# Sparse cross attention, 64 batches: one more pipeline stage, with a new order of work on all engines

## The reference, cut to what matters

```python
q = split_heads(x @ w_q);  k, v = split_heads(text @ w_k), split_heads(text @ w_v)
out_text = softmax(q k^T / 4) v
out_ip   = softmax(q k_ip^T / 4 + mask_ip) v_ip      # mask_ip: a box per query, 8 columns
out = (merge(out_text) + merge(out_ip)) @ w_out + b_out + x
```

## Time and profile before

| | us |
|---|---|
| median of 3 runs | 1598.76 (1596.06 to 1602.39) |
| profiled execution | 1604.02 |
| its span, first to last instruction | 1602.1 |
| PE busy | 1385.2 (86%) |
| PE weight loads busy | 1266.7 (79%) |
| DVE busy | 1173.1 (73%) |
| ACT busy | 848.4 (53%) |
| POOL busy | 806.3 (50%) |
| mean granted TensorE clock | 0.959 |

### The profile page before, as it was taken

The page is one execution under the profiler, slowest core; times in us unless marked ns, Lnnn a source line. Parts: engine busy times, 40 slices in busy tenths (PEclk is TensorE's granted clock), DMA queues, the critical chain, the costliest instruction groups (busy, mean ns, idle before and its releaser), DMA issues.

```text
span 1602.1 us, 48578 instructions
## 1 busy us (share of the span) xinstructions
PE 1385.2 (86%) x15736; PEld 1266.7 (79%) x15736; DVE 1173.1 (73%) x3602; ACT 848.4 (53%) x2064; POOL 806.3 (50%) x1038
## 2 busy tenths in 40 slices
PE   6778775899989989989998998998998998999997
PEld 5778774788878878878887887887887888888886
DVE  5368443788878877877887886887887886888885
ACT  3344432555555555555555555555554555555553
POOL 0132220555555555555555555555555555555554
PEclk9899995999999999999999999999999999999998
DMA  5788994343333443433433333433433333444331
GB/s 136 112 199 171 187 168 88 84 93 94 92 74 89 93 95 88 93 93 87 93 93 86 93 93 71 94 92 88 93 93 91 94 93 85 93 94 93 94 76 37
DMA packets 361215, 159.25 MB, mean 99 GB/s; under 512 B 298417, under 2 KB 350514, under 8 KB 359666
## 3 DMA queue, kind: packets, MB, share of 16 engines
q1 hardware_dynamic: 355826, 134.83, 37.3%
q10 hardware_dynamic: 5120, 20.98, 6.3%
HBM read 91.69 MB, written 43.05 MB: 84 GB/s over the span
## 4 chain that ended last, share of the span: by engine, by line
PE 42%; DVE 14%; issue 14%; ACT 10%; ACTq 2%; DVEq 1%; POOL 1%; DMA 0%; POOLq 0%; SPq 0%
PE ps_o L928 9%; PE ps_a L852 9%; PE ps_b L852 8%; PE ps_m L876 5%; PE ps_s L899 4%; PE ps_s L905 4%; ACT prob_hi L1037 3%; DVE values L1145 3%; ACT xT_hi L1007 2%; DVE y L1135 2%; PE ps_b L887 2%; DVE stats L1104 2%; ACT aT_hi L1025 2%; ACTq L1018 2%; DVE inv L1110 1%
## 5 line engine op out<-in xcount | busy, mean ns | idle before, releaser
L1197 POOL TENSOR_TENSOR prob_lo<-prob,prob_hi 128x512 f16<-128x512 f32 (+1 forms) x448 | 488.9, 1091 | 169.5 <-ACT prob_hi L1037 169.3
L1208 POOL TENSOR_TENSOR attn<-heads 128x128 f32<-128x128 f32 (+1 forms) x512 | 271.9, 541 | 440.0 <-DVE heads L1118 440.0
L1036 ACT ACTIVATE prob<-ps_s 128x512 f32<-128x512 f32 (+1 forms) x448 | 254.0, 567 | 388.6 <-PE ps_s L905 379.9
L928 PE MATMUL ps_o<-values,prob_hi 128*128 128x64 bf16 (+7 forms) x4992 | 311.3, 196 | 3.8 <-DVE values L1145 1.8
L928 PE MATMUL ps_o<-values,prob_lo 128*128 128x68 bf16 (+7 forms) x3328 | 300.2, 196 | 0.0
L928 PEld LDWEIGHTS ps_o<-values,prob_hi 128*128 128x128 f16 x4992 | 268.8, 99 | 25.8 <-DVE values L1145 2.0
L1100 DVE TENSOR_REDUCE stats<-ps_m 128x4 f32<-128x276 f32 x640 | 277.0, 433 | 0.0
L899 PE MATMUL ps_s<-q_hi_lo,keys 128*128 128x256 f32 x960 | 260.3, 305 | 0.0
L1037 ACT ACTIVATE prob_hi<-ps_s 128x512 f16<-128x512 f32 (+1 forms) x448 | 251.4, 561 | 0.0
L905 PE MATMUL ps_s<-q_hi_extra,keys 128*128 128x256 f32 x960 | 246.1, 292 | 0.9 <-ACT q_hi_extra L1052 0.3
L876 PE MATMUL ps_m<-keys,q_hi_lo 128*128 128x308 f32 x640 | 219.2, 360 | 12.7 <-DVE stats L1100 4.8
(11 more groups left out here) (165 smaller groups left out, 3032.5 us busy)
## 6 DMA issues: line engine op xcount, KB each, us to landing
x_in<-in_x_dram SPq DMA_DIRECT2D x64, 320.0 KB, 3.3
q_hi_extra<-q_hi_lo ACTq DMA_DIRECT2D x64, 320.0 KB, 3.3
x_keep<-in_x_dram SPq DMA_DIRECT2D x64, 320.0 KB, 3.2
out_dram<-y SPq DMA_DIRECT2D x128, 160.0 KB, 1.8
k_scratch<-k_stage SPq DMA_DIRECT2D x16, 770.0 KB, 5.8
keys<-k_scratch SPq DMA_DIRECT2D x256, 48.1 KB, 2.0
ctx_in<-in_ctx_dram SPq DMA_DIRECT2D x64, 128.0 KB, 3.1
v_scratch<-v_stage SPq DMA_DIRECT2D x64, 120.0 KB, 5.5
```

The lines of the kernel that those rows point to most:

```text
L928: last = mm(o[:, :, oo:oo + w], stat, v[:, :, a:a + w], start=first, stop=False, skip_group_check=True)
L1036: nc.scalar.activation(prob[:, s, 0:w], ps_s[RING[s]][:, 0:w], ACT.Exp)
L1197: nc.gpsimd.tensor_tensor(prob_lo[par(b)][:, s, 0:w], prob[:, s, 0:w], prob_hi[par(b)][:, s, 0:w], ALU.subtract).then_inc(s_lo, 1)
L1208: last = nc.gpsimd.tensor_tensor(attn[:, t, c0:c0 + nh * DH].rearrange("p (h c) -> p h c", c=DH), hv[:, :, 0, :], hv[:, :, 1, :], ALU.add)
```

## The change

Five batches are now in work in one step in place of four. A new stage **E** takes `x_transpose` and `project` of batch **b+2**; stage **A** keeps the maxima, the `stats_transpose` and the extra rows of b+1. B, C and D work on the batches they had. To hold q over the longer time, `q_hi_lo` has three buffers (`third`). `sched` begins one step earlier, at -2; the loop still has nine rounds of six steps.

The order in a step is new on all engines. On PE each slot is `scores(s)`, two blocks of maxima (slots 0 to 4, no table), the item of E, C or D, then `sum_heads(s)`. `stats_transpose` stands in slot 5, ahead of `sum_heads(5)` and `scores(6)`. On ACT the extra rows follow the fifth pair of exponentials and precede the last, and `x_hi(0)` stands behind the first pair. On DVE the maxima come first in a slot, `invert` and `norm` stand directly behind each other, and the three pieces of `spread_values` stand in slots 1, 3 and 4 in place of 4, 5 and 6. `project` now writes `ps_b` three times (before: `ps_b` twice, `ps_a` once) and both `attn_transpose` write `ps_a` (before: one each). The copy of q moves from ACT's queue to SP's, at the head of the step.

The diff, cut to its core:

```diff
-MAXIMA = [[], [], [0, 1, 2], [3, 4, 5], [6, 7], [8, 9], []]
...
-            q_hl = [sb(f"q_hi_lo{q}", [P, QUADS, S], f32r, st) for q in range(2)]
+            q_hl = [sb(f"q_hi_lo{q}", [P, QUADS, S], f32r, st) for q in range(3)]
...
-                first, last = min(4, NB), max(NB - 2, min(4, NB))
+                first, last = min(4, NB), max(NB - 4, min(4, NB))
                 last -= (last - first) % 6
-                for b in range(-1, first):
+                for b in range(-2, first):
...
+                    def copy_q(b):
+                        sp.wait_ge(s_qhi, at(b, QUADS, QUADS))
+                        wait(sp, s_sc, b, PAIRS, -PAIRS)
+                        sp.dma_start(q_ex[par(b)][0:QD].rearrange("p q s -> p (q s)").bitcast(fp32),
+                                     q_hl[third(b)][0:QD].rearrange("p q s -> p (q s)").bitcast(fp32)).then_inc(s_qx[par(b)], 16)
...
+                        if A:
+                            copy_q(off(b, 1))
+                        if n is None or n + 4 < NB:
+                            sp.wait_ge(s_xt, at(b, NT, 3 * NT))
+                            load_x(off(b, 4))
                         if Ds:
                             store(off(b, -2), 1)
                         if Bs:
                             load_residual(b)
-                        if n is None or n + 2 < NB:
-                            sp.wait_ge(s_xt, at(b, NT, NT))
-                            load_x(off(b, 2))
                         if Cs:
                             store(off(b, -1), 0)
-                        if n is None or n + 2 < NB:
+                        if n is None or 0 <= n < NB - 2:
                             sp.wait_ge(s_vx, at(b, 3, 3))
...
                         if m == 2:
-
-                            wait(pe, s_yr, b, NT, -2 * NT)
-                        ps = (ps_b, ps_b, ps_a)[m]
+                            pe.wait_ge(s_qlo, at(b, QUADS, 4))
+                        ps = ps_b
...
-                        if t == 0:
-                            pe.wait_ge(s_qlo, at(b, QUADS, h4 + 1))
                         if n == 0:
+                            pe.wait_ge(s_qlo, at(b, QUADS, QUADS))
...
-                    def stats_transpose(b, n):
+                    def stats_transpose(b, E):
                         pe.wait_ge(s_ip, at(b, NT, NT))
 
-                        if n is None or n >= 1:
-                            pe.wait_ge(s_alo, at(b, NT, 1 - 2 * NT))
+                        if E:
+                            pe.wait_ge(s_qlo, at(b, QUADS, 2 * QUADS))
...
+                    def attn_transpose(b, t, E, Ds):
                         pe.wait_ge(s_at, at(b, UNITS, 3 * t + 3))
-                        ps = (ps_b, ps_a)[t]
...
-                        if t == 0 and A:
-                            pe.wait_ge(s_qlo, at(b, QUADS, QUADS * 2 + 5))
-                        elif t == 0:
-                            wait(pe, s_yr, b, NT, 0)
...
-                        A, Bs, Cs, Ds = has(n)
-                        a, c = off(b, 1), off(b, -1)
-                        d = off(b, -2)
+                        E, A, Bs, Cs, Ds = has(n)
+                        e, a, c, d = off(b, 2), off(b, 1), off(b, -1), off(b, -2)
                         for s in range(PAIRS):
-                            if A and s == 0:
-                                x_transpose(a, 0, n)
                             if Bs:
                                 scores(b, s)
-                            if A and s == 0:
-                                x_transpose(a, 1, n)
+                            if A and s < QUADS:
+                                max_scores(a, 2 * s)
+                                max_scores(a, 2 * s + 1)
+                            if E and s == 0:
+                                x_transpose(e, 0, n)
+                                x_transpose(e, 1, n)
                             if Ds and s == 1:
-                                attn_transpose(d, 1, A, n)
-                            if Ds and s == 2:
-                                project_out(d, 1, A)
-                            if A and s in (1, 2, 3):
-                                project(a, s - 1)
-                            if A and MAXIMA[s]:
-                                max_scores(a, MAXIMA[s][0])
-                            if Cs:
-                                if s == 4:
-                                    attn_transpose(c, 0, A, n)
-                                if s == 5:
-                                    project_out(c, 0, A)
-                                if s < UNITS:
-                                    sum_heads(c, s)
-                            if A:
-                                for m in MAXIMA[s][1:]:
-                                    max_scores(a, m)
-                        if A:
-                            stats_transpose(a, n)
+                                attn_transpose(d, 1, E, Ds)
+                            if E and s == 2:
+                                project(e, 0)
+                            if Ds and s == 3:
+                                project_out(d, 1)
+                            if E and s == 3:
+                                project(e, 1)
+                            if Cs and s == 4:
+                                attn_transpose(c, 0, E, Ds)
+                            if E and s == 4:
+                                project(e, 2)
+                            if Cs and s == 5:
+                                project_out(c, 0)
+                            if A and s == 5:
+                                stats_transpose(a, E)
...
-                        def copy_q():
-                            act.wait_ge(s_qhi, at(a, QUADS, QUADS))
-                            act.dma_start(q_ex[par(a)][0:QD].rearrange("p q s -> p (q s)").bitcast(fp32),
-                                          q_hl[par(a)][0:QD].rearrange("p q s -> p (q s)").bitcast(fp32)).then_inc(s_qx[par(a)], 16)
...
+                        def extra():
+                            act.wait_ge(s_et, at(a, 1, 1))
+                            nc.scalar.copy(q_ex[par(a)][QD:P, 0, :], ps_b[QD:P, 0:S]).then_inc(s_ex, 1)
+                            nc.scalar.copy(q_ex[par(a)][QD:P, 1:QUADS, :],
+                                           ps_b[QD:P, 0:S].rearrange("p (o s) -> p o s", o=1).broadcast_to([QD, QUADS - 1, S])
+                                           ).then_inc(s_ex, 1)
...
                                 nc.scalar.activation(prob_hi[par(b)][:, s, 0:w], ps_s[RING[s]][:, 0:w], ACT.Exp
                                                      ).then_inc(s_hi, 1)
-                            if A:
-                                if s == 0:
-                                    x_hi(1)
+                            if E and s == 0:
+                                x_hi(0)
+                                x_hi(1)
                             if Ds and s == 1:
-                                a_hi(off(b, -2), 1)
-                            if A and s in (1, 2, 3):
-                                q_hi(s - 1)
-                            if A and s == 4:
-                                copy_q()
+                                a_hi(d, 1)
+                            if E and s in (2, 3):
+                                q_hi(s - 2)
                             if Cs and s == 4:
                                 a_hi(c, 0)
-                        if A:
-                            act.wait_ge(s_et, at(a, 1, 1))
-                            nc.scalar.copy(q_ex[par(a)][QD:P, 0, :], ps_b[QD:P, 0:S]).then_inc(s_ex, 1)
-                            nc.scalar.copy(q_ex[par(a)][QD:P, 1:QUADS, :],
-                                           ps_b[QD:P, 0:S].rearrange("p (o s) -> p o s", o=1).broadcast_to([QD, QUADS - 1, S])
-                                           ).then_inc(s_ex, 1)
+                            if E and s == 4:
+                                q_hi(2)
+                            if A and s == 5:
+                                extra()
 
                     sched(act, step)
 
...
-                        d = off(b, -2)
                         for s in range(PAIRS):
-                            if A and s == 0:
+                            if A and s < QUADS:
+                                maxima(2 * s)
+                                maxima(2 * s + 1)
+                            if E and s == 0:
                                 x_lo(0)
                                 x_lo(1)
                             if Ds and s == 1:
                                 a_lo(d, 1)
-                            if Ds and s == 2:
+                            if E and s == 2:
+                                q_lo(0)
+                            if Ds and s == 3:
                                 finish(d, 1)
-                            if A and MAXIMA[s]:
-                                maxima(MAXIMA[s][0])
-                            if A and s in (1, 2, 3):
```

(62 more changed lines are left out.)

48 lines of the change are left out of this document (21 added, 27 removed).

## The result

The changed kernel takes 1548.62 us (median of 4 runs, 1545.3 to 1550.35) against 1598.8 before: a ratio of 0.968, with a 95% interval of 0.966 to 0.971. The forecast was 1553: 2.9% less forecast, 3.2% measured. The profiled execution took 1550.35 us, its span is 1548.6.

A forecast was written before the change was run, and what follows sets the result against it. PE was taken as the bound, with DVE close behind. 275 to the first transposes + 63 x 19.1 (1203) + 8 x 5.1 (41) + 37 = 1556 us span, forecast median 1553 us; range 1535 to 1572, 8 in 10: 1508 to 1594.

The forecast's parts named there:

- The step: One loop step: 16.8 us of PE work plus waits of 1.55 and 0.8, 19.1 us against 19.97.
- What goes: PE's old waits for the transposed maxima (1.24 us a step) and ps_b (0.4), and project(0)'s for xT, vanish.
- The new waits: Two new PE waits a step: 1.55 us in slot 1 and 0.8 us at project_out(0).
- The second wait: PE's project_out(0) waits for DVE's a_lo(0), 0.8 us a step.
- The branch: The loop's branch adds 5.1 us to a step, bounds 3.8 and 5.5, eight times (41 us).
- The ends: First transposes of maxima near 275 us, 9 later than before; 37 us behind the last, 0.8 added.
- The copy of q: On SP behind the loads, last issued 9.3 us into the step; there near 13, wanted at 19.1; cost nothing.
- ACT's detour is hidden: Rival: x tiles copied in time, the first wait shrinks; step 18.55 us, 1518 us in all; chance 0.22.
- the first wait: PE's sum_heads(1) waits in slot 1 for DVE's norm(0), about 1.55 us; 1.0 if ACT's detour costs nothing.
- DVE loses to POOL: Rival: DVE's spread is held up by POOL's subtraction, 0.58 us; step 19.7, 1590 us; chance 0.12.
- Lockstep over `ps_o`: Rival: each slot lasts as long as PE's or DVE's longer share, plus handover; step 21.2, 1685 us; chance 0.09.
- The gap between `invert` and `norm`: On DVE, 0.1 us, formerly filled by a block of maxima, now paid six times a step.

The follow-up runs named there:

- experiment 1: Changed kernel, but ACT copies both x tiles before the step's first pair of exponentials, not after it: 1500.15 us, ratio 0.937.
- experiment 4: Changed kernel with the maxima's transposes on PE and ACT's extra rows back at the end of the step: 1590.93 us, ratio 0.993.
- experiment 5: Changed kernel with only ACT's extra rows moved behind the last pair of exponentials; PE still transposes in slot 5: 1602.05 us, ratio 1.003.
- experiment 3: Changed kernel with the three spreads back in slots 4, 5 and 6 in place of 1, 3 and 4: 1534.11 us, ratio 0.959.
- experiment 6: Kernel of experiment 1 with the spread of slot 3 put ahead of q_lo(1) on DVE: 1514.46 us, ratio 0.947.
- experiment 7: Kernel of experiment 6 with invert(0) and norm(0) between the two low parts of x on DVE: 1512.75 us, ratio 0.946.
- experiment 8: Changed kernel with the spreads in slots 3, 4 and 5: 1544.79 us, ratio 0.967.
- experiment 2: Changed kernel, but DVE takes invert(0) and norm(0) before the two low parts of x: 1529.32 us, ratio 0.956.
- experiment 9: Kernel of experiment 1 with each slot's second block of maxima on DVE moved behind invert and the slot's other item: 1625.36 us, ratio 1.015.

## Why the prediction was right

**The step** was walked at 19.1 us and is 19.08, and it closes by the mechanism named. The first x tile was put at 2.26 us after the step's first scores (measured 2.23), DVE's idle time there at 1 us (0.89), the end of `norm(0)` at 5.12 (its start at 4.69 and 0.42 long: 5.11). Experiments 1, 4 and 5 move that tile by -0.94, +0.79 and +0.94 us, and the step moves by -0.94, +0.73 and +0.92: the link is close to one to one, in both directions. DVE, which I wanted idle for at least 1 us a step, was busy 16.55 of 19.10 us in the one from 904.4 to 923.5.

**What goes** went: the 1.24 us for the maxima, the 0.4 us for `ps_b`. Experiment 5 adds a point that the prediction made only in part. The gain hangs on the extra rows standing ahead of the last exponentials on ACT; placed behind, they cost it all. The prediction has "The extra rows are formed while PE runs `sum_heads(5)` and `scores(6)`" among several reasons; the experiments show that nothing is gained without it. They do not show that it is enough: the fifth stage was in place in all of them.

**The new waits** were sized 1.55 and 0.8 us. PE's weight loads in slot 1:

```profile
908.86 0.20 PEld L953 LDWEIGHTS ps_a<-ident,attn 128*128 128x128 f32 x2 [0.38 <-DVE xT L1069]
...
910.44 0.14 PEld L935 LDWEIGHTS ps_o<-values,prob_hi 128*128 128x128 f16 x3 [1.27 <-DVE heads L1113]
```

The second wait measured 0.79 (42.5 us in 54). The first is 1.27 in this step, and 0.38 us stand just ahead of it in a wait that the working has no term for: `attn_transpose` may not overwrite `ps_a` before DVE is through with x. This wait and the first hang on the same late x tiles. Then PE's own work is 19.08 - 0.38 - 1.27 - 0.79 = 16.6 us, where I had 16.8; experiment 1, with 18.14 - 0.68 - 0.79 = 16.7, gives the same. So each term is right within 0.3 us, with 0.38 us of waiting one item earlier on PE than I had it.

**The branch** was kept at 5.1 us, and here two errors partly cancel, which is luck. From the first to the last transposes there are 1514.5 - 276.3 = 1238.2 us. The eight distances across the branch are 23.97 to 25.23 us, 24.58 on average: 5.5 more than a step, 0.4 more than I had and at my upper bound (before: 25.09, 5.1 more). But the first two distances and the last are 14.77, 18.00 and 15.81, since the steps at either end are not full: 8.7 us less than three full steps, which the working did not take off. The branch did take away the wait for `norm`, as the prediction says. PE stands instead 3.1 us ahead of `scores(0)` and 1.1 us more at the x tiles without a releaser, and the granted clock in that step is 0.86, as before. What causes the second piece is open. **The ends**: first transposes at 276.3 (275), and 1548.6 - 1514.5 = 34.1 us behind the last (37). All together the span is 1548.6 us for a forecast of 1556.

**The copy of q** was put near 9.3 us and 13 us landed. In the trace of the changed kernel SP issues it at 914.45, 9.2 us after the step's start, and copies take 3.5 us to land. No wait of the loop is put down to it.

**The rivals.** ACT's detour is hidden: no, the tile came at 2.23 and DVE stood for it. But with the detour taken out (experiment 1) the step is 18.14, not 18.55: I had put the first wait at 1.0 us then, and it is 0.68, with the 0.38 for x gone as well. DVE loses to POOL: not in this kernel, where the narrow spread takes 526 ns and the wide ones 774. The narrow one did lose in the kernel before, with 652 ns (wide: 773). It happens in experiments 3, 6, 7 and 8, so it was right to price it and right that the new places avoid it. Lockstep over `ps_o`: PE waits for `norm` 48 times in the loop, once a step and not in five or six slots, and experiments 2 and 7 gain 0.37 us and nothing by freeing the bank sooner. The gap between `invert` and `norm`, which I counted against the change, was left: filling it with the slot's second maxima costs 2 us a step through `ps_m` (experiment 9). A filling that leaves those maxima ahead of the slot's other item was not tried.

What stays open: what sets the 18.14 us of experiment 1. DVE stands only about 0.6 us of such a step for other engines, and PE still waits 0.68 and 0.79 us; no experiment that I made on top of it was faster.

## What to carry to other kernels

When engines work from written orders, walk one step with each engine's start times from the trace, and repeat it until it closes on itself; the item to look for is the short one that stands behind long ones on an engine with time to spare. ACT was 55% busy here, and the place of a few copies on it was worth 3.5% of the time in one direction (experiment 5) and 3.1% in the other (experiment 1). Before reordering DVE, list for each bank which instruction frees it and how far DVE runs behind PE: a block that looks done a slot ago may not be.

## What the runs showed of the hardware that I had not expected

A spread that begins after POOL's subtraction is held up in turn: 1.23 us where it takes 0.77, with 0.57 us between the two starts. The end of the spread is then 0.63 us behind POOL's recorded end (939.85 + 1.17). Over the loop the median of this distance is 0.64 us for the wide spread, whether it starts 0.57 us (experiment 6) or 0.62 us (experiment 3) after the subtraction, and 0.39 us for the narrow one in experiments 3 and 8 and in the kernel before, with 0.77 and 0.53 us recorded alone. So the spread is not slowed in proportion: it ends a fixed time behind POOL, 0.13 us short of its own recorded length.
